# A fused attention and expert layer: the tables loaded in two parts, head steps put elsewhere in the order, gating written in place, scatter sources loaded ahead, and scatters and gathers paced by TensorE's tiles

## The reference, cut to what matters

```python
def attention(x, k, Wh, wg, wo, gamma, beta):        # x, k: 4 x 512 x 512, 4 heads of 128
    Q, K, V = x@Wh, k@Wh, k@Wh                         # per head
    A = maximum(abs((Q@K.T / sqrt(128) * decay).sum(axis=batch)), 1)   # one A per head, for all batches
    O = A @ V
    Y = (O - mean) / sqrt(var + 1e-3) * gamma + beta   # over all 512 columns
    return relu(x@wg) * Y @ wo
def experts(x):                                        # 2048 tokens, 16 experts of width 352
    scores = softmax(x@Wg.T); top 2 of 4 groups, then top 4 experts of them
    y = sum over the 4 of score * (silu(x@W1[e].T) * (x@W3[e].T)) @ W2[e].T
    z = the same form with shared weights of width 704, for every token
    return y + z
x = x + attention(layernorm(x), ctx)
x = x + experts(layernorm(x))
```

## Time and profile before

| | |
|---|---|
| median of 3 runs | 988.34 us (988.08 to 989.44) |
| the profiled execution | 987.74 us, its span 986.1 us |
| TensorE busy (matmul) | 936.0 us, 95% of the span |
| VectorE, ScalarE, GpSimd busy | 531.2, 330.7, 481.5 us |
| mean granted TensorE clock | 0.991 |

### The profile page before, as it was taken

The page is one execution under the profiler, slowest core; times in us unless marked ns, Lnnn a source line. Parts: engine busy times, 40 slices in busy tenths (PEclk is TensorE's granted clock), DMA queues, the critical chain, the costliest instruction groups (busy, mean ns, idle before and its releaser), DMA issues.

```text
span 986.1 us, 18867 instructions
## 1 busy us (share of the span) xinstructions
PE 936.0 (95%) x5216; PEld 833.3 (85%) x5217; DVE 531.2 (54%) x1033; ACT 330.7 (34%) x695; POOL 481.5 (49%) x345
## 2 busy tenths in 40 slices
PE   6999998899899958999999999999999999999998
PEld 5767776687799948999999999999999999989886
DVE  5657878888976523333333333333333333337997
ACT  4554444353334212332223333333332233332221
POOL 1126666773167672535255554355555450007772
PEclk9999999999999988999999999999999999999999
DMA  6749943655587754245534554555555222238994
GB/s 204 255 149 401 391 185 113 219 182 160 180 275 274 276 217 161 84 168 176 176 131 166 169 167 151 173 173 173 167 173 176 85 85 85 85 98 243 299 279 126
DMA packets 118419, 183.62 MB, mean 186 GB/s; under 512 B 13552, under 2 KB 70896, under 8 KB 115696
## 3 DMA queue, kind: packets, MB, share of 16 engines
q1 hardware_dynamic: 104480, 103.76, 32.5%
q0 software_dynamic: 13904, 79.44, 23.3%
HBM read 111.85 MB, written 71.30 MB: 186 GB/s over the span
## 4 chain that ended last, share of the span: by engine, by line
PE 77%; DVE 13%; DMA 3%; issue 3%; ACT 2%; POOL 1%; SPq 1%; DVEq 0%; POOLq 0%; ACTq 0%
PE ps L998 14%; PE ps L1000 14%; PE ps L999 14%; PE ps L1050 8%; PE ps L1052 7%; PE ps L1051 7%; PE ps L833 4%; DMA gin<-gate_d 2%; DVE gate_out L1149 2%; PE ps L871 2%; DVE res L1521 2%; DVE ctx_sum L1146 1%; PE ps L900 1%; PE ps L898 1%; PE ps L899 1%
## 5 line engine op out<-in xcount | busy, mean ns | idle before, releaser
L998 PE MATMUL ps<-whi,xhi 128*128 (+1 forms) x896 | 300.0, 335 | 11.6 <-POOL wlo L511 10.9
L1000 PE MATMUL ps<-whi,xlo 128*128 (+1 forms) x896 | 289.9, 324 | 0.0
L999 PE MATMUL ps<-wlo,xhi 128*128 (+1 forms) x896 | 289.3, 323 | 0.0
L998 PEld LDWEIGHTS ps<-whi,xhi 128*128 128x128 f32 x896 | 169.4, 189 | 12.5 <-issue 11.9
L999 PEld LDWEIGHTS ps<-wlo,xhi 128*128 128x128 f32 x896 | 170.4, 190 | 0.0
L1000 PEld LDWEIGHTS ps<-whi,xlo 128*128 128x128 f32 x896 | 168.9, 189 | 0.0
L1296 DVE TENSOR_TENSOR hx<-ps,sg 128x352 f32<-128x352 f32 x112 | 58.7, 524 | 185.0 <-ACT sg L746 184.9
L746 ACT ACTIVATE sg<-ps 128x352 f32<-128x352 f32 x112 | 52.0, 465 | 303.4 <-PE ps L1000 303.4
L1318 DVE TENSOR_TENSOR hlo<-ps,hhi 128x384 fp32r<-128x384 f32 x112 | 62.3, 556 | 169.4 <-ACT hhi L789 169.2
L509 POOL CAST whi<-raw 128x2816 fp32r<-128x2816 f32 x16 | 40.5, 2532 | 208.5 <-PE ps L1000 208.5
L1050 PE MATMUL ps<-whi,hhi 128*128 (+1 forms) x333 | 132.8, 399 | 2.9 <-DVE hlo L1318 2.9
(11 more groups left out here) (176 smaller groups left out, 1413.1 us busy)
## 6 DMA issues: line engine op xcount, KB each, us to landing
raw<-wexp_in POOLq DMA_DIRECT2D x18, 2176.0 KB, 9.5
xslot_d<-zero SPq DMA_DIRECT2D x10, 2048.0 KB, 21.7
xg<-xslot_d SPq DMA_DIRECT2D x320, 64.0 KB
yslot_d<-ysb SPq DMA_DIRECT2D x80, 256.0 KB, 2.1
xg<-xn_d SPq DMA_DIRECT2D x128, 64.0 KB
xq<-x_in SPq DMA_DIRECT2D x16, 256.0 KB, 3.6
gate_d<-gate_out SPq DMA_DIRECT2D x16, 256.0 KB, 2.8
gin<-gate_d SPq DMA_DIRECT2D x16, 256.0 KB, 3.4
```

The costliest lines, as they stand in the source:

```text
L998: pe.matmul(ps[:, 2 + m, 0:INTER], xh, wh, start=(k == 0), stop=False)
L999: pe.matmul(ps[:, 2 + m, 0:INTER], xh, wl, start=False, stop=False)
L1000: mm = pe.matmul(ps[:, 2 + m, 0:INTER], xl, wh, start=False, stop=(k == KT - 1))
```

## The change

The tables come in two loads: the unit matrix and the epsilons (130 columns) where all stood, the rest behind the loads of token tiles 2 and 3, with a semaphore `t_loaded` of its own. TensorE multiplies zeros three times before anything else. ScalarE rounds the gate weights in two pairs, the first pair earlier. In the heads, `gram(h+1)` and the column sums stand between blocks of `scores(h)`. The gated tile is written over `o_sb`, and `load_gate` waits for `gated`. The scatter sources are loaded three tiles ahead of SyncE's step, where they were two tiles behind; the load of weight set 3 leaves the scatters and goes behind `split(2)`; each tile's scatters, and each tile's gathers, first wait for a count of `mm1`. TensorE's projection stage and GpSimd's first two weight sets are written out without a loop.

```diff
-            sp.dma_start(const[:, :], tables).then_inc(c_loaded, 16)
+            sp.dma_start(const[:, 0:C_REST], tables[:, 0:C_REST]).then_inc(c_loaded, 16)
...
+                if type(t) is int and t == XR - 1:
+                    sp.dma_start(const[:, C_REST:C_ALL], tables[:, C_REST:C_ALL]).then_inc(t_loaded, 16)
...  load_gate
-                    sp.wait_ge(a_tr, t - 1)
+                    sp.wait_ge(gated, t - 1)
...
-            pipeline(sp, NT, [(XG, next_tile), (-2, load_scat)], ring=XG)
+            pipeline(sp, NT, [(XG, next_tile), (3, load_scat)], ring=XG)
...  scatters on GpSimd
-                if t == NT - XR:
-                    pool.wait_ge(first_lo, 2 * NT)
-                    pool.dma_start(raw[:, 1, :], wexp[3, :, :]).then_inc(raw_loaded[1], 16)
+                pool.wait_ge(mm1, 2 + (26 * t + 51) // 32)
...  set_and_next, behind split(o + 2)
+                if type(o) is int and o == 0:
+                    pool.wait_ge(first_lo, 2 * NT)
+                    pool.dma_start(raw[:, 1, :], wexp[3, :, :]).then_inc(raw_loaded[1], 16)
...
-            pipeline(pool, NW - 4, [(0, set_and_next)], ramp=0)
+            pipeline(pool, NW - 4, [(0, set_and_next)])
...  gathers on GpSimd
+                pool.wait_ge(mm1, 2 + NT + NR + (26 * t + 38) // 32)
...  ScalarE: wg_split(ks) over a part of the weights
+                if type(t) is int and t == 0:
+                    wg_split((0, 1))          # behind std_1(0)
-                    wg_split()
+                    wg_split((2, 3))
...  ScalarE, head: the copy of the column sums moves from ahead of the scores to
+                    if j == 1:
+                        act.wait_ge(sum_mm, h + 1)
+                        act.wait_ge(o_ready, ST * h)
+                        act.activation(v_sum, ps[:, 6, :], ACT.Copy).then_inc(sum_ready, 1)
...  TensorE
+            pe.wait_ge(zero_ready, 1)
+            for i in range(3):
+                pe.matmul(ps[:, 7, :], zero[:, 0:P], zero[:, :], start=True, stop=True)
...
+            def v_rows(h):
+                pe.wait_ge(o_ready, max(ST * h - 1, 0))
                 pe.wait_ge(sum_w, B * (h + 1))
                 pe.matmul(ps[:, 6, :], ones, w_sum, start=True, stop=True).then_inc(sum_mm, 1)
...  scores
+                    if j == 0:
+                        v_rows(h)
+                    if j == 1 and h + 1 < H:
+                        gram(h + 1)
...
-                transposes(ps[:, p, :], gin[:, p, :], KT, a_tr)
+                transposes(ps[:, p, :], o_sb[:, t, :], KT, a_tr)
...
-            pipeline(pe, NT, [(1, tr_a), (0, proj), (-2, tr_b_on), (-3, router_on)], ring=XR)
+            pipeline(pe, NT, [(1, tr_a), (0, proj), (-2, tr_b_on), (-3, router_on)], ramp=NT, ring=XR)
...  VectorE: gram(h+1) behind its second block of scores(h), as on TensorE
-                dve.tensor_tensor(gin[:, p:p + 1, :], gin[:, p:p + 1, :], o_sb[:, bass.ds(t, 1), :], ALU.mult).then_inc(gated, 1)
+                dve.tensor_tensor(o_sb[:, bass.ds(t, 1), :], gin[:, p:p + 1, :], o_sb[:, bass.ds(t, 1), :], ALU.mult).then_inc(gated, 1)
```

More of the change, by code:

```diff
@@ L42 @@
 LAG, PACE = 3, 5
-C_ID, C_UP, C_ONE = 0, 128, 256
-C_IOTA, C_CAP, C_LT, C_LG, C_TILE, C_KDEC = 384, 400, 416, 672, 688, 768
-C_EPS = 784
+C_ID, C_EPS, C_REST = 0, 128, 130
+C_UP, C_ONE = 130, 258
+C_IOTA, C_CAP, C_LT, C_LG, C_TILE, C_KDEC = 386, 402, 418, 674, 690, 770
 C_ALL = 786
@@ L609, in _, with wg_split @@
             act.wait_ge(c_loaded, 16)
-            def wg_split():
-                for k in range(KT):
+            def wg_split(ks):
+                for k in ks:
                     act.wait_ge(w1_loaded[k], 16)
@@ L663, in head @@
                     act.activation(v_hi[:, tt, :], ps[:, V_BANK[tt], :], ACT.Copy).then_inc(v_ready, 1)
-                act.wait_ge(sum_mm, h + 1)
-                act.wait_ge(o_ready, ST * h)
-                act.activation(v_sum, ps[:, 6, :], ACT.Copy).then_inc(sum_ready, 1)
                 act.wait_ge(w3_loaded, 48)
@@ L679, in head @@
                     ctx_high(h + 1)
+            act.wait_ge(t_loaded, 16)
             ctx_high(0)
@@ L861, in _, with gram @@
             pe.wait_ge(s1_xnT, NT)
-            def queries(h):
+            pe.wait_ge(t_loaded, 16)
+            def gram(h):
                 wT = head_in[:, h % 2, HC_WT:HC_WT + HD]
@@ L867, in queries @@
                 pe.matmul(ps[:, 0, 0:HD], wT, wT, start=True, stop=True).then_inc(g_mm, 1)
+            def queries(h):
                 pe.wait_ge(g_ready, h + 1)
@@ L882, in values @@
                     mm.then_inc(v_mm, 1)
-                if h:
-                    pe.wait_ge(o_ready, ST * h - 1)
+            def v_rows(h):
+                pe.wait_ge(o_ready, max(ST * h - 1, 0))
                 pe.wait_ge(sum_w, B * (h + 1))
@@ L933, in first_tr_a @@
                 pe.wait_ge(sum_ready, H)
-                transposes(ps[:, 0, :], gin[:, 0, :], KT, a_tr)
+                transposes(ps[:, 0, :], o_sb[:, 0, :], KT, a_tr)
+            gram(0)
             queries(0)
@@ L1129, in _, with gram @@
             dve.wait_ge(qdec_loaded, 16)
-            def queries(h):
+            dve.wait_ge(t_loaded, 16)
+            def gram(h):
                 dve.wait_ge(g_mm, h + 1)
@@ L1199, in first_scaled @@
                 dve.wait_ge(o_gated, 1)
-                dve.scalar_tensor_tensor(gin[:, 0, :], gin[:, 0, :], sd3[:, 1, 0:1], gate_beta, ALU.mult, ALU.add).then_inc(gated, 1)
+                dve.scalar_tensor_tensor(o_sb[:, 0, :], gin[:, 0, :], sd3[:, 1, 0:1], gate_beta, ALU.mult, ALU.add).then_inc(gated, 1)
             def a_low(t, r, turn):
```

5 lines of the change are left out of this document (3 added, 2 removed).

## The result

The changed kernel takes **978.73 us** (median of 4 runs, 975.78 to 980.28) where the kernel before takes 988.89 beside it: ratio 0.989 with the 95% interval [0.9865, 0.9916]. Its profiled execution took 977.7 us, span 976.1. The forecast was 971.5 with the range 967 to 976.5: faster, as forecast, but by 10.0 us between the two profiled executions instead of 16.8. The time lies above the range.

What follows compares the result with a forecast made beforehand. TensorE, busy in 95% of the span, bounds the kernel; its idle time lies at stage borders. 987.74 - 1.5 - 4.6 - 0.7 - 10.0 = 970.9, with 0.6 for the median 971.5 us; range 967 to 976.5.

Steps and rivals of the forecast that it cites:

- The hole, -10.0: Between last shared and first expert tile: earlier scatters let TensorE start 8.1 us sooner, plus 1.9 from its clock.
- a clock that stays: After the hole: TensorE may keep its clock, giving 2.5 us more instead of the 1.9 taken; bound -10.6.
- The heads, -4.6: In the heads: TensorE's waits for column sums' input, `g_sb` and `o_ready` go, not replaced; bounds -1.3 and -5.3.
- rival 1: Heads stay latency-bound: GpSimd's remainders or VectorE's v remainder come later, waits return under other names; 974.8, chance 0.15.
- The beginning, -1.5: At the start: VectorE starts 1.0 us earlier, a faster TensorE gives at most 0.5; bounds 0 and -2.4.
- Gating, -0.7: Gated tiles: the load for tile 2 goes out 0.7 us sooner, ahead of the transposes; bounds 0 and -2.
- Permits at nothing: Scatters and gathers: their waits for `mm1` cost nothing; for scatters the cover is 4.4 us at tile 3.
- rival 5: Scatters: the pacing by `mm1` does something, a late one holds the scatters, but no time hangs on it; no chance given.
- Rivals 2 and 4: 2: shared tiles, SyncE blocks itself, 975.5, chance 0.10. 4: slow scatters make it slower than before, chance 0.03.
- rival 4: Scatters beside VectorE's routing take longer, their end passes the hole again; at 1.65 us each 993; chance 0.03.

Runs made afterwards that it cites:

- e5: The changed kernel with nothing edited, measured again in a quiet session: 979.03 us, ratio to the kernel before 0.9907.
- e18: The kernel before with only scatter sources three tiles ahead and set 3's load moved, no waits for `mm1`, quiet session: 978.42 us, ratio 0.9915.
- e3: The changed kernel without the waits of scatters and gathers for `mm1`, late session: 1047.71 us, ratio to the kernel before 1.0193.
- e13: The changed kernel with nothing edited, in a late session: 1031.9 us, ratio to the kernel before 0.9978.
- e14: The kernel before with nothing edited, in a late session: 1032.43 us with the profile, session median 1033.42.
- e4: The changed kernel with the heads' four multiplies moved from VectorE to ScalarE, late session: 1028.2 us, ratio to the kernel before 0.9991.
- e12: The changed kernel with multiplies on ScalarE, decay table loaded in four parts, no products of zeros, late session: 1025.46 us, ratio to the kernel before 0.9891.

## Why the prediction was wrong, step by step

- **The hole, -10.0:** right. From the third shared tile to the transposes behind the first expert tile (L844 at 368.66, before L833 at 378.76) it is 99.98 us instead of 110.50: -10.5, the bound for a clock that stays. In e5 and e18 the first expert product lasts 0.66 us and the same stretch takes 101.4: -9.0, with the clock lower for a while. `xlo`, sources without a wait, 5.2 us of scatters per tile (forecast 5.1) and the load of set 3 all came as chained.
- **The heads, -4.6:** the step that failed. The pair of traces gives -0.52, outside the bounds of -1.3 and -5.3. The prediction said "VectorE's last remainder of v ends at 106.8 [...] 0.5 us of cover" and took the waits "as gone, not replaced". I had chained v's remainder to its own predecessors and moved them all with TensorE. But the four multiplies ahead of it are tied to GpSimd's run, and that run did not move: GpSimd was busy without a break from 89.4 to 100.7 in both. So v's remainder started at 104.30 and 104.31; TensorE, now ready for the weight product at 105.52, waited 1.41 us for it. These new waits leave 3.0 us of the 4.6 where the holds are equal and short. The rest is head 3: there the hold was 7.14 us instead of 4.01, the sums waited, ScalarE's copy and the attention remainder came late, TensorE idled 2.24 us and then ran at its lower clock for some 3.5 (0.63 in the window), 2.5 us together. That a short hold before met a long one after is the luck of this pair; on average the new order gives 3.2. The sign was there: in the trace of before these multiplies have a mean of 1.09 us, and most last 0.27. This was rival 1, with a cause that it did not name.
- **The beginning, -1.5:** mis-sized, and nothing of it is left. VectorE's early start came, but the second tile was only 0.1 us earlier at the median, and the gate's store behind 1 MB of decay table then cost TensorE 0.57 + 0.50 us at 45; the heads began 0.25 later in the pair, 0.6 on average. I had followed the stage to its second tile only. Not priced: what the next transfer stands behind.
- **Gating, -0.7:** not seen. The load goes out at 165.18, ahead of the transposes, and lands 7.71 us later, where before it took 6.72 from 166.49; the gated product starts at 172.99, 7.46 us after the transposes began, before 7.50. Its landing, not its issue, ends the wait. The stage took 103.15 us where it was 102.46; over all traces 101.9 to 104.9, with no order between old and new. Why that spreads was not tried.
- **Permits at nothing:** right in quiet sessions, and rival 5's "No time hangs on it" wrong elsewhere: 18.7 us. Rivals 2 and 4 did not come beside the forecast; VectorE never waited for `xg` in the shared tiles. In late sessions the scatter part without permits was slower than the kernel before, but with a hole of 3.0 us and scatters of 0.97 us at the median: the time went into late signals within the tiles, not where rival 4 had it.

## What to carry to other kernels

Before moving work past an engine, look at instructions whose mean is several times their median: here that time was a wait inside the instruction, and it ended where another engine decided. A cover computed along one engine's chain is worth nothing if that chain is tied to a third engine; giving the four multiplies to ScalarE, on top of the new order, won what the new order alone could not. One pair of traces can't size a term that is smaller than the spread of its stage: here the pair said +0.4 for three terms of which one was worth 3 us on average. And follow an earlier start to the end of its stage, through the transfers, before counting it.

## What the hardware showed that was not expected

In late sessions, waits for TensorE end with a releaser that the trace does not know ("remote"). Timeline of e3, changed kernel without permits: the last product of a shared tile, the last scatter before a pause, ScalarE, TensorE.

```profile
274.17 0.32 PE L1018 MATMUL ps<-whi,xlo 128*128 128x352 f32 x1
...
298.24 0.97 POOL L569 DMA_INDIRECT xslot_d<-scat,sloti  x1 [0.30 <-issue]
...
303.28 0.46 ACT L752 ACTIVATE sg<-ps 128x352 f32<-128x352 f32 x1 [31.41 <-remote]
...
304.36 0.90 PE L842 MATMUL ps<-const,hx 128*128 128x128 f32 x3 [27.78 <-DVE hx L1320]
```

The product that ScalarE waits for ends at 274.5 by the trace; ScalarE goes on 28.8 us later, some 4 us after a row of 28 scatters without a pause has stopped. With permits (e13) ScalarE and GpSimd wait for the same signal and are let go together:

```profile
305.94 0.46 ACT L754 ACTIVATE sg<-ps 128x352 f32<-128x352 f32 x1 [5.67 <-remote]
...
306.18 0.97 POOL L570 DMA_INDIRECT xslot_d<-scat,sloti  x1 [2.25 <-remote]
```

GpSimd's last scatter before it began at 302.96. All such waits, on ScalarE, VectorE and GpSimd, are for TensorE, and all lie in the stages with scatters or gathers; the quiet sessions have none. The kernel before has them too in a late session (e14), up to 8.8 us. So it looks as if TensorE's signals (or the ends of its products, which the trace models) are held back while indirect transfers are queued, and as if a permit bounds this because a late permit also stops the transfers. The bound is shown for the scatters: the longest delay there is 8.4 to 9.2 us in the three late traces with permits (e4, e12, e13) and 30.1 to 31.6 in the seven that load the sources ahead and have none. Among the gathers it is not: 9.3 to 10.5 with permits, 9.3 to 12.4 in the same seven. The path by which transfers hold signals back, and what makes a session late, stay open.
